# Routed experts: the routing weight applied where a token's rows are added, instead of where each expert tile is written

## What is computed

```python
logits = h @ router_w.T                      # 1024 tokens, 16 experts
probs = softmax(logits)
top_vals, top_idx = top_k(probs, 4)
top_vals = top_vals / maximum(top_vals.sum(-1), 1e-9)
comb = zeros((N, 16)).at[arange(N)[:, None], top_idx].add(top_vals)
g = einsum('nh,ehi->eni', h, w_gate); u = einsum('nh,ehi->eni', h, w_up)
y = einsum('eni,eih->enh', silu(g) * u, w_down)
routed = einsum('enh,ne->nh', y, comb)
shared = silu(h @ sh_gate) * (h @ sh_up) @ sh_down
x = x + routed + sigmoid(h @ sh_gate_w) * shared
```

## Time and profile before

| | us |
|---|---|
| median of 3 runs | 581.49 |
| lowest, highest | 581.3, 582.16 |
| the profiled execution | 581.71 |
| its span, first to last instruction | 579.9 |

### The profile page before, as it was taken

The page is one execution under the profiler, slowest core; times in us unless marked ns, Lnnn a source line. Parts: engine busy times, 40 slices in busy tenths (PEclk is TensorE's granted clock), DMA queues, the critical chain, the costliest instruction groups (busy, mean ns, idle before and its releaser), DMA issues.

```text
span 579.9 us, 11051 instructions
## 1 busy us (share of the span) xinstructions
PE 495.6 (85%) x3338; PEld 436.4 (75%) x3338; DVE 450.2 (78%) x1358; ACT 357.8 (62%) x903; POOL 318.6 (55%) x298
## 2 busy tenths in 40 slices
PE   0599979998889898995659999999899999588894
PEld 0478757877788887994449999999799998346673
DVE  4779967875877786756598889999989887769674
ACT  2345547253558676763237877878688889666643
POOL 2547671014467886415767788788577773363100
PEclk9989999999999998996597999999999999989997
DMA  8144454312364555545820000000000000000000
GB/s 276 38 126 129 131 152 126 90 58 67 98 195 111 188 187 161 144 131 145 284 62 19 28 21 19 29 19 1 2 1 2 2 1 2 0 1 9 11 28 27
DMA packets 27961, 45.24 MB, mean 78 GB/s; under 512 B 5697, under 2 KB 18849, under 8 KB 27265
## 3 DMA queue, kind: packets, MB, share of 16 engines
q1 hardware_dynamic: 21056, 28.15, 15.8%
q0 software_dynamic: 3792, 10.74, 7.2%
q10 hardware_dynamic: 3056, 5.65, 3.1%
HBM read 34.63 MB, written 8.85 MB: 75 GB/s over the span
## 4 chain that ended last, share of the span: by engine, by line
PE 48%; DVE 24%; issue 10%; DMA 7%; ACT 6%; POOL 5%; SPq 0%; DVEq 0%; ACTq 0%; POOLq 0%
PE bank L415 8%; PE bank L416 8%; PE bank L417 8%; PE bank L1080 8%; PE bank L1521 5%; DMA bw<-bits_dram 2%; DVE pT_lo L1580 2%; DVE sc L2081 1%; ACT pr L956 1%; PE bank L1476 1%; DVE X L1632 1%; DMA inb<-rows_kept,row_of 1%; DMA seg<-seg_dram 1%; DVE asel L1632 1%; PE bank L1282 1%
## 5 line engine op out<-in xcount | busy, mean ns | idle before, releaser
L584 POOL DMA_INDIRECT inb<-rows_kept,row_of x47 | 47.4, 1008 | 37.8 <-PE bank L1080 20.8
L956 ACT ACTIVATE pr<-sc,smin 128x256 f32<-128x256 f32 x128 | 63.3, 502 | 0.0
L661 POOL TENSOR_TENSOR Q_lo<-Q,Q_hi 128x512 fp32r<-128x512 f32 x32 | 41.5, 1297 | 22.7 <-ACT Q_hi L695 22.1
L2081 DVE CUSTOM_DVE_ANT_0 sc<-bank,bias 128x256 f32<-128x256 f32 x128 | 46.5, 418 | 0.1
L648 POOL TENSOR_TENSOR pr<-pr,srec 128x512 f32<-128x512 f32 x32 | 33.4, 1042 | 21.6 <-DVE srec L2088 21.6
L1580 DVE TENSOR_TENSOR pT_lo<-bank,pT_hi 128x512 fp32r<-128x512 f32 x64 | 41.1, 683 | 5.0 <-ACT pT_hi L695 5.0
L695 ACT ACTIVATE pT_hi<-bank 128x512 fp32r<-128x512 f32 x64 | 35.0, 595 | 13.6 <-PE bank L1080 13.3
L612 POOL DMA_INDIRECT yk<-slots_y,slot x32 | 33.7, 1052 | 14.0 <-issue 5.8
L655 POOL TENSOR_TENSOR Q<-Q,rot 128x512 f32<-128x512 f32 x32 | 41.2, 1286 | 0.0
L1080 PE MATMUL bank<-const,pr 128*128 128x128 f32 x256 | 34.8, 279 | 6.6 <-POOL pr L648 6.5
L965 ACT ACTIVATE pr<-pr,srec 128x256 f32<-128x256 f32 x64 | 29.1, 502 | 16.7 <-DVE srec L2088 16.7
(11 more groups left out here) (346 smaller groups left out, 1939.5 us busy)
## 6 DMA issues: line engine op xcount, KB each, us to landing
slots_y<-yb SPq DMA_DIRECT2D x47, 128.0 KB
wg_raw<-gate_up_dram SPq DMA_DIRECT2D x22, 256.0 KB, 2.8
bw<-bits_dram ACTq DMA_DIRECT2D x3, 1024.0 KB
wd_raw<-down_dram SPq DMA_DIRECT2D x16, 128.0 KB, 2.1
wo<-wo_dram SPq DMA_DIRECT2D x2, 1024.0 KB, 6.7
wd_raw<-down_dram SPq DMA_DIRECT2D x30, 64.0 KB, 2.2
gu_raw<-gate_up_dram SPq DMA_DIRECT2D x6, 256.0 KB, 3.5
X<-x_dram SPq DMA_DIRECT2D x2, 512.0 KB, 6.8
```

The source lines that it names most:

```text
L584: pool.indirect_dma_start(inb[:, j % NIN, :], None, rows_d, bass.IndirectOffsetOnAxis(row_of[:, j:j + 1], 0)).then_inc(slots_in[j % NIN], 16)
L661: pool.tensor_tensor(Q_lo[:, i % 2, :], Q[:, i % 2, :], Q_hi[:, i % 2, :].bitcast(F32), ALU.subtract).then_inc(queries_low_g, 1)
L956: e = act.activation(pr[:, i % 2, z, :], sc[:, i % 2, z, :], ACT.Exp, bias=smin[:, i % 2, z:z + 1], scale=-1.0, accum_out=ssum[:, i % 2, z ...
L2081: dve.tensor_tensor_reduce(sc[:, r, z, :], bank[2 + h][:, u * S:(u + 1) * S], bias[:, TB * b_ + u, :], 1.0, 3.0e38, ALU.add, ALU.min, smin ...
```

## The change

The results of the expert tiles are stored unscaled. The pick per routed tile goes, with `picked`, `share`, `tile_p`, their semaphore and the waits on it, and so does the `comb` matrix and its store; rows in `rows_kept` have 256 words (1024 bytes). `shares` computes `rank_w` instead, the normalised weight of each token's k-th choice, from the four largest values that `top8` holds already. `combine` uses four fused multiply-and-adds, X = yk * weight + X, for two adds among the rows and one into X. The wait for the stores of rows moves from `shares` to `tiles_and_lanes`, which begins to write where the stored rows lay.

```diff
-ROWW = D + E
-    rows_d = nc.dram_tensor("rows_kept", (N, ROWW), F32, kind="Internal").ap()
+    rows_d = nc.dram_tensor("rows_kept", (N, D), F32, kind="Internal").ap()
-        picked = sb("picked", [P, 2, E])
-        share = sb("share", [P, 8])
+        rank_w = sb("rank_w", [P, NT, TOPK])
...
             def gather_slots(j):
                 if j >= NIN:
                     pool.wait_ge(slots_turned_p, j - NIN + 1)
-                    pool.wait_ge(slot_share_v, j - NIN + 1)
...
-                if v == 5:
-                    act.wait_ge(routing_v, COMB)
-                    act.dma_start(rows_d[:, D:ROWW].rearrange("(t p) e -> p t e", p=P), comb[:, :, :]
-                                  ).then_inc(rows_kept[0], 16)
...
             def slots_copy(j):
                 act.wait_ge(slots_down_p, j + 1)
-                act.wait_ge(slot_share_v, j + 1)
                 if j >= 3:
                     act.wait_ge(slots_out[j % 3], out_count(j - 3))
-                act.activation(yb[:, j % 3, :], bank[4 + j % 2][:, 0:D], ACT.Copy, scale=share[:, j % 8:j % 8 + 1]
-                               ).then_inc(slots_copied_a, 1)
+                copy(yb[:, j % 3, :], bank[4 + j % 2][:, 0:D]).then_inc(slots_copied_a, 1)
...
-                dve.tensor_scalar(tile_p[:, :], bank[3][:, 384:384 + SLOTT], E - 1.0, None, ALU.min)
...
             def shares():
 
+                link(dve.tensor_reduce(rsum[:, :], prob[:, :, :], AX_X, ALU.add))
+                link(dve.reciprocal(rsum[:, :], rsum[:, :]))
+                link(dve.tensor_tensor(rank_w[:, :, :], top8[:, :, 0:TOPK],
+                                       rsum[:, :].unsqueeze(2).to_broadcast([P, NT, TOPK]), ALU.mult))
+                link(dve.tensor_reduce(rsum[:, :], rank_w[:, :, :], AX_X, ALU.add))
+                link(dve.tensor_scalar(rsum[:, :], rsum[:, :], 1e-9, None, ALU.max))
+                link(dve.reciprocal(rsum[:, :], rsum[:, :]))
+                dve.tensor_tensor(rank_w[:, :, :], rank_w[:, :, :],
+                                  rsum[:, :].unsqueeze(2).to_broadcast([P, NT, TOPK]), ALU.mult)
...
-                link(dve.tensor_reduce(rsum[:, :], prob[:, :, :], AX_X, ALU.add))
-                link(dve.reciprocal(rsum[:, :], rsum[:, :]))
-                link(dve.tensor_tensor(prob[:, :, :], prob[:, :, :], rsum[:, :].unsqueeze(2).to_broadcast([P, NT, E]),
-                                       ALU.mult))
-                link(dve.tensor_tensor(comb[:, :, :], prob[:, :, :], member[:, :, :], ALU.mult))
-                link(dve.tensor_reduce(rsum[:, :], comb[:, :, :], AX_X, ALU.add))
-                link(dve.tensor_scalar(rsum[:, :], rsum[:, :], 1e-9, None, ALU.max))
-                link(dve.reciprocal(rsum[:, :], rsum[:, :]))
-                dve.tensor_tensor(comb[:, :, :], comb[:, :, :], rsum[:, :].unsqueeze(2).to_broadcast([P, NT, E]),
-                                  ALU.mult).then_inc(routing_v, 1)
...
-            def slot_share(j):
-
-                if j >= 8:
-                    dve.wait_ge(slots_copied_a, j - 7)
-                link(dve.scalar_tensor_tensor(out=picked[:, j % 2, :], in0=const[:, K_IOTA:K_IOTA + E],
-                                              scalar=tile_p[:, j:j + 1], in1=inb[:, j % NIN, D:ROWW],
-                                              op0=ALU.is_equal, op1=ALU.mult))
-                dve.tensor_reduce(share[:, j % 8:j % 8 + 1], picked[:, j % 2, :], AX_X, ALU.add).then_inc(slot_share_v, 1)
...
-                link(dve.tensor_tensor(yk[:, r, 0:2, :], yk[:, r, 0:2, :], yk[:, r, 2:4, :], ALU.add))
-                link(dve.tensor_tensor(yk[:, r, 0, :], yk[:, r, 0, :], yk[:, r, 1, :], ALU.add))
-                link(dve.tensor_tensor(X[:, t, :], X[:, t, :], yk[:, r, 0, :], ALU.add))
+                for k in range(TOPK):
+                    link(dve.scalar_tensor_tensor(out=X[:, t, :], in0=yk[:, r, k, :], scalar=rank_w[:, t, k:k + 1],
+                                                  in1=X[:, t, :], op0=ALU.mult, op1=ALU.add))
```

More of the change, by code:

```diff
@@ L216, in build @@
                         "hit": ([P, 2, TOPK, SLOTT], BF16), "pt": ([P, 2, TOPK, 2, SLOTT], BF16),
-                        "comb": ([P, NT, E], F32), "lane": ([P, NT * TOPK], F32), "tileno": ([P, NT * TOPK], F32),
-                        "row_f": ([P, SLOTT], F32), "skip3": ([P, 128], F32), "tile_p": ([P, SLOTT], F32)},
+                        "skip4": ([P, P], F32), "lane": ([P, NT * TOPK], F32), "tileno": ([P, NT * TOPK], F32),
+                        "row_f": ([P, SLOTT], F32)},
                        {"bits": ([P, 3, 2048], BF16), "bias": ([P, NT, S], F32),
@@ L223, in build @@
                         "sil": ([P, 2, I_MOE], F32), "hd": ([P, 2, KD * P], F32), "sbias": ([P, S], F32),
-                        "inb": ([P, NIN, ROWW], F32)},
+                        "inb": ([P, NIN, D], F32)},
                        {"skip": ([P, 5120], F32), "kr": ([KVC, 4, P], F32), "kr_hi": ([KVC, 4, P], F32R),
@@ L246, in build @@
                            ).split()]
-        lanes, hit, pt, comb, lane, tileno, row_f, tile_p = [
-            m[k] for k in "lanes hit pt comb lane tileno row_f tile_p".split()]
+        lanes, hit, pt, lane, tileno, row_f = [m[k] for k in "lanes hit pt lane tileno row_f".split()]
         x_in = [sem(f"x_in{i}") for i in range(2)]
@@ L290, in build @@
              "down_high_a down_low_v gate_p up_p gate_silu_a hidden_v hidden_high_a hidden_low_v down_p x_shared_v "
-             "hit_v place_v placed_p slot_share_v slots_turned_p slots_high_a slots_low_v slots_gate_up_p slots_silu_a slots_hidden_v hidden_turned_p "
+             "hit_v place_v placed_p slots_turned_p slots_high_a slots_low_v slots_gate_up_p slots_silu_a slots_hidden_v hidden_turned_p "
              "turned_high_a turned_low_v slots_down_p slots_copied_a "
@@ L325, in build @@
         UNITS = 2 * C_SH
-        LOGITS, LOGITS_SHIFTED, MEMBER, TILES_OF, COMB, SLOT_OF, PASSED, TILE_EXPERT, ROW_OF = range(1, 10)
+        LOGITS, LOGITS_SHIFTED, MEMBER, TILES_OF, SLOT_OF, PASSED, TILE_EXPERT, ROW_OF = range(1, 9)
         COUNTED, RANKED, PASSED_SUM = range(1, 4)
@@ L601, in _ @@
             for i in range(4):
-                pool.wait_ge(rows_kept[i], 32 if i else 48)
+                pool.wait_ge(rows_kept[i], 32)
             for j in range(TILES):
@@ L791, in _ @@
                     hi_h(0, i - 4, bank[6], H_hi)
-                    act.dma_start(rows_d[(i - 4) * P:(i - 3) * P, 0:D], hn[:, (i - 4) % 4, :]
+                    act.dma_start(rows_d[(i - 4) * P:(i - 3) * P, :], hn[:, (i - 4) % 4, :]
                                   ).then_inc(rows_kept[(i - 4) % 4], 16)
@@ L1826, in shares @@
             def shares():
-                for i in range(4):
-                    dve.wait_ge(rows_kept[i], 32)
                 link(dve.tensor_reduce(rsum[:, :], prob[:, :, :], AX_X, ALU.add))
                 link(dve.reciprocal(rsum[:, :], rsum[:, :]))
-                link(dve.tensor_tensor(prob[:, :, :], prob[:, :, :], rsum[:, :].unsqueeze(2).to_broadcast([P, NT, E]),
-                                       ALU.mult))
-                link(dve.tensor_tensor(comb[:, :, :], prob[:, :, :], member[:, :, :], ALU.mult))
-                link(dve.tensor_reduce(rsum[:, :], comb[:, :, :], AX_X, ALU.add))
+                link(dve.tensor_tensor(rank_w[:, :, :], top8[:, :, 0:TOPK],
+                                       rsum[:, :].unsqueeze(2).to_broadcast([P, NT, TOPK]), ALU.mult))
+                link(dve.tensor_reduce(rsum[:, :], rank_w[:, :, :], AX_X, ALU.add))
                 link(dve.tensor_scalar(rsum[:, :], rsum[:, :], 1e-9, None, ALU.max))
                 link(dve.reciprocal(rsum[:, :], rsum[:, :]))
-                dve.tensor_tensor(comb[:, :, :], comb[:, :, :], rsum[:, :].unsqueeze(2).to_broadcast([P, NT, E]),
-                                  ALU.mult).then_inc(routing_v, 1)
+                dve.tensor_tensor(rank_w[:, :, :], rank_w[:, :, :],
+                                  rsum[:, :].unsqueeze(2).to_broadcast([P, NT, TOPK]), ALU.mult)
                 dve.wait_ge(logits_exp_a, 2)
@@ L1843, in tiles_and_lanes @@
             def tiles_and_lanes():
+                for i in range(4):
+                    dve.wait_ge(rows_kept[i], 32)
                 link(dve.tensor_scalar(tileno[:, :], slotf[:, :], 1.0 / P, -(P - 1.0) / (2 * P), ALU.mult, ALU.add))
```

5 lines of the change are left out of this document (1 added, 4 removed).

## The result

The changed kernel takes 585.59 us (median of 20 runs, 582.19 to 589.6); the kernel before, run beside it 20 times, 581.92. The ratio is 1.0065, with a 95% interval of 1.0045 to 1.0086: slower by 3.8 us, between 2.6 and 5.0. Ratios are taken over runs made beside each other, without the few slow ones, and need not equal the ratio of two medians. The forecast was +1.2, 582.7 us, with a range that ended at 585.0; direction right, size too small by a factor of three. A second comparison, of 12 runs against 23, gave 586.02 and 1.0041 [1.0007, 1.0075]. The two agree within their intervals; the first is the narrower. By the second alone, +2.4 us, the kernel would lie inside the range. The profiled executions are 5.2 us apart, 585.1 us of span after against 579.9 before.

What follows compares the result with a forecast made beforehand. TensorE bounds the routed-expert loop; VectorE is the path where TensorE idles behind combines. Terms +3.2 - 0.65 - 0.35 - 0.6 - 0.4 = +1.2 us on 581.49 give 582.7 us, range 579.2 to 585.0.

Steps and rivals of the forecast that it cites:

- The fused form: Eight combines: four linked fused operations take 2.04 us against 1.64 for three adds, +0.40 each, +3.2 us in all.
- No cover: Combines stand where TensorE already idles, with no spare time later, so all 8 x 0.40 us counts.
- Collisions: Combine operations stretched beside GpSimd: 8 more chances at 0.09 us each, 0 to +0.7 us, upper end only.
- Routing arithmetic: VectorE work before the loop gets 0.65 us shorter, shrinking TensorE's idle 1.19 us before `place`: -0.65 us.
- The loop: Loop over 47 tiles: third group -0.35, ScalarE's copy out -0.6, gathered rows -0.4; together -1.35 us.
- gathered rows: Loop: rows of 1024 B instead of 1088 B let 1 MB loads 1 and 2 land earlier: -0.4 us (0 to -0.7).
- bit load 1: Loop: the sum waits for the 1 MB load of `bw`, not for the pick, so removing the pick gains 0.
- third group: Loop: the third sum, directly behind the pick, and gather 32 both come earlier: -0.35 us (0 to -0.35).
- the copy: Loop: ScalarE's copy out without pointer scale takes 0.385 instead of 0.478 us: -0.6 us (0 to -0.9).
- Rival A: Loop loses its third lump if gather 32 lands before VectorE's third sum ends: 1.8 us more, sum -0.6; chance 0.2.
- Rival C: GpSimd collisions come (+0.7) and gains of ScalarE and loads fail: +3.3 us, 584.8; chance 0.12.

## Why the prediction was right or wrong

The stages, cut at the first and last copy out, the first turn of attention, the turn behind combine 4 (342.60 in the earlier trace rows) and the turn that starts the last stage (506.15 before, 507.94 after). Each line uses the profiles whose code in that stage is that of before or of after:

| stage | before: range, mean (profiles) | after: range, mean (profiles) | difference | forecast |
|---|---|---|---|---|
| up to the first copy out | 154.0-154.8, 154.3 (5) | 152.0-155.1, 153.9 (9) | -0.5 | -0.65 |
| loop | 103.6-106.0, 104.9 (4) | 101.0-106.2, 102.8 (8) | -2.1 | -1.35 |
| to the first turn (combines 0, 1) | 17.9-19.2, 18.6 (7) | 19.4-20.7, 20.1 (8) | +1.4 | +0.8 |
| start of attention (2, 3, 4) | 63.3-64.9, 64.1 (6) | 66.4-68.1, 67.1 (5) | +3.1 | +1.2 |
| the other slots (5, 6, 7) | 163.5-164.0, 163.7 (5) | 164.1-164.3, 164.2 (7) | +0.5 | +1.2 |
| last stage | 73.7-76.0, 75.0 (6) | 75.0-77.2, 75.7 (8) | +0.7 | 0 |
| sum | | | +3.1 | +1.2 |

Up to the loop the ranges overlap; in the three stages with combines they don't. The last stage holds no line of the change; its +0.7 is the scatter of the clock. With it or without it the sum agrees with the +2.4 and +3.8 us of the two comparisons. The prediction's sentence that the stages of the first profile are those of the median fails for that stage: at 73.7 us it is the shortest of all.

- **The fused form, +0.40 a combine: right.** 0.485 us an operation, 2.04 for four, 2.08 from the first to `bn_stats`; the reason, the pointer scalar as in the earlier trace rows, is right too. The estimate from the Trainium skill ("VectorE: DVE Perf Modes", the SBUF-source errata: +0.19 a combine) fits the form with a constant, 0.425 us an operation and 1.80 for four, not the form with a pointer.
- **No cover: right, with one exception.** TensorE's idle times grew by 0.82 over combines 0 and 1, and at combines 4 to 6 from 0.2-0.4 to 0.6-0.8 each. Combine 7 lost nothing, since the 1.22 us add of the earlier trace rows was not stretched again (the idle time there fell from 1.91 to 1.66): the three slots cost 0.5, not 1.2.
- **Collisions, 0 to +0.7 and left out of the sum: this is the step that failed.** I had priced them as an average over all adds, 0.09 us each. But a collision is not a lottery over 24 adds: in slot 2 GpSimd's order is fixed against VectorE's, and the earlier trace rows had shown one stretched add of 1.83 us there. A fourth operation behind it had to start later than any add had, and GpSimd's gather and subtraction stood there. The combine took 4.77 us instead of the 2.78 of the adds: 1.6 us on top of the 0.40, in every one of five profiles, where the whole term was put at no more than 0.7. With the 1.6 us alone the forecast would be +2.8 instead of +1.2. The rule that I had quoted (the Trainium skill, "SBUF — State Buffer", "Who interferes with whom": such an instruction and GpSimd's exclude each other for their whole length) is what the trace shows for the first operation, which ends 0.29 us after GpSimd's. For the fourth it fits only in part: it waited out a subtraction that began 0.53 us after it, and an operation of the same form ran through a gather in slot 3 in 0.48 us. I had the rule, and priced it at a mean.
- **Routing arithmetic, -0.65: not contradicted.** The mean is -0.5, and TensorE's idle 1.19 us became 0.42 in the recorded profile; but profiles with the code of before show 0.2 to 1.3 there (seven, mean 1.0) and those with the code of after 0.3 to 1.25 (nine, mean 0.7). The stage is too noisy to call it shown.
- **The loop, -1.35: direction right, terms wrong.** The gathered rows (-0.4) are worth nothing. The statement that bit load 1 waits for its transfer and not for the pick was read rightly from the earlier trace rows and was still wrong as a price: the transfer itself came earlier once the picks were gone. The first group won 1.7 us in the mean where I had 0.4. The third group won 1.1 in the mean, but 0.5 of it is the one profile of before whose clock fell; without it the gain is 0.6, and 0.35 for the pick and 0.2 for the copy was the forecast. It takes both. The second group lost 0.8 in the mean, where the load and the clock scattered.
- **Rival A: its deciding event came, its price is not the change's.** In all eight profiles without pick and scale the wait for gather 32 no longer ends behind the third sum: TensorE's longest wait there is the 0.8 us for the sum, where before it was 1.2 to 1.7 us for the gather in three of four profiles. The 1.8 us that Rival A added are the fall of the clock to 0.83 in the earlier trace rows, which only one of the four profiles of before had: that profile took 27.9 us for the group, the others 25.8 to 25.9. Between the two recorded profiles the lump went whole; in the mean most of it was not there to be won.
- **Before the first turn** 0.6 us more than the combines explain are lost between the last copy and the turn. That is open.
- **Rival C** (+3.3, 584.8) was the one that came nearest, and by its decisive point: a fused operation inside a GpSimd operation. Its size of 0.7 was too small, and its other half, that the loop's gains fail, was not so; that its time is near is in part luck.

The range ended at 585.0 because its upper end took the mean price of the collisions too. With the one stretched operation at its full length, what GpSimd has queued there (a gather of 1.0 us and a subtraction of 1.3, so up to 2.3 us), it would have ended near 587.

## What to carry to other kernels

Where two engines exclude each other, don't price the exclusion as a mean over all operations. Look at the slot where the trace already shows a stretched operation, write down what the other engine has queued behind, and ask where the new operations will start against it; in slot 2 a shift of 0.15 us, and with it the change of form, decided over 1.8. Then read several profiles of each kernel: a fall of the clock that only one has can pass for a lump that the change could win. A chain that gets one link more is judged by when its last link starts. And a wait that "ends on a transfer" is no proof that the engine work beside it is free: the transfer landed earlier in the profiles in which that work was gone.

## What the runs showed of the hardware

- The scalar operand as a pointer costs a fused multiply-and-add of 128x256 fp32 with both inputs in SBUF 0.06 us: 0.485 us against 0.425 with a constant. ScalarE's copy of 128x256 pays 0.09 for it: 0.478 against 0.389.
- VectorE operations with two SBUF inputs beside GpSimd's issue of an indirect gather (0.96 to 0.99 us long in these three cases): started 0.49 us into it, with a GpSimd subtraction right behind, one took 2.10 us and ended 0.29 us after the subtraction; started 0.68 us into it, with the subtraction right behind, 1.86 us, again to 0.29 us after it; started 0.69 us into it, with the subtraction 1 us behind, 0.48 us. One with a constant, started 0.33 us into it, took 0.43 us, and the gather's issue took 1.16 us.
- A 1 MB load beside the loop landed 5.4 to 5.6 us after its issue in one place and 6.3 to 7.0 in another (four profiles of the changed loop); in three more profiles of that loop the sum that waits for it in the second place started 8.0 to 8.2 us after the issue.
- Behind the same idle time of 5.71 us of TensorE, executions differed in the granted clock between 8 and 14 us after work began again: 1.00 in one execution of the kernel before, 0.72 in another, with TensorE busy for 5.9 of 6 us in both. The stage took 73.7 us without this fall and 75.0 to 77.2 with it.
- ScalarE ran 47 more operations of 0.20 us in the loop (busy 75.5 of 101.8 us, against 71.7 of 105.2 in the kernel before), and the loop did not get longer; with 48 registers loaded on the same engine right before the loop, the first copy out came 1.7 us later than with the same loads made earlier.
